# Causal attention in a decoder kernel: a ring of four PSUM banks becomes two tiles of two banks, with one maximum instruction for two heads' pieces

## What is computed

```
q, k, v = layer_norm(x) @ Wqkv + bqkv          # 16 heads of 16 features
s = q @ k.T * 16 ** -0.5                       # per head, 1024 x 1024
s = where(key <= query, s, -inf)
x = x + softmax(s) @ v @ Wout + bout
```

## Time and profile before

| | us |
|---|---|
| median of 3 runs | 1536.88 |
| lowest and highest | 1535.32, 1543.87 |
| the profiled execution | 1545.4 |
| its span | 1543.6 |
| TensorE busy in the span | 1452.9 |
| VectorE busy | 986.8 |
| ScalarE busy | 753.1 |
| GpSimd busy | 494.0 |
| the 304 maxima (L2303), busy | 179.6 |
| the 304 exponentials (L2255), busy | 155.2 |

### The profile page before, as it was taken

The page is one execution under the profiler, slowest core; times in us unless marked ns, Lnnn a source line. Parts: engine busy times, 40 slices in busy tenths (PEclk is TensorE's granted clock), DMA queues, the critical chain, the costliest instruction groups (busy, mean ns, idle before and its releaser), DMA issues. The chain is left out here.

```text
span 1543.6 us, 19029 instructions
## 1 busy us (share of the span) xinstructions
PE 1452.9 (94%) x6910; PEld 848.3 (55%) x6914; DVE 986.8 (64%) x1506; ACT 753.1 (49%) x1237; POOL 494.0 (32%) x410
## 2 busy tenths in 40 slices
PE   6999999989999999888999998898889999999998
PEld 3757764432232265453444443322568888888886
DVE  5774243768877743548888783676677575664853
ACT  5466344443334451543666565434655545445442
POOL 0046420123132410343111112102136655655562
PEclk9999997999999999998999999899999999999999
DMA  7000000000000000083535300000313223223201
GB/s 293 1 0 0 1 1 4 0 1 1 0 1 1 1 0 0 1 164 42 125 51 74 42 3 1 4 1 4 133 42 110 69 83 100 78 74 104 73 10 55
DMA packets 39044, 67.55 MB, mean 44 GB/s; under 512 B 3944, under 2 KB 19368, under 8 KB 38568
## 3 DMA queue, kind: packets, MB, share of 16 engines
q1 hardware_dynamic: 38952, 66.33, 16.1%
HBM read 57.80 MB, written 8.39 MB: 43 GB/s over the span
## 5 line engine op out<-in xcount | busy, mean ns | idle before, releaser
L2255 ACT ACTIVATE arena<-psum 128x512 f32<-128x512 f32 (+1 forms) x304 | 155.2, 583 | 109.9 <-PE psum L2100 109.2
L2303 DVE TENSOR_REDUCE b_mx<-psum 128x1 f32<-128x512 f32 (+3 forms) x304 | 179.6, 650 | 45.0 <-PE psum L2078 36.9
L3047 POOL TENSOR_TENSOR m_w_rest<-m_w,m_w_high 128x512 fp32r<-128x512 f32 (+1 forms) x88 | 111.6, 1270 | 155.6 <-ACT m_w_high L3246 155.6
L3497 DVE TENSOR_TENSOR m_hidden<-m_gelu,psum 128x512 f32<-128x512 f32 (+1 forms) x88 | 60.4, 686 | 148.6 <-ACT m_gelu L3338 124.4
L3140 PE MATMUL psum<-m_x_high,m_w_high 128*128 128x512 f32 (+1 forms) x352 | 138.4, 393 | 3.2 <-issue 3.2
L3053 POOL TENSOR_TENSOR m_h_rest<-m_hidden,m_h_high 128x512 fp32r<-128x512 f32 (+1 forms) x88 | 122.4, 1390 | 58.9 <-ACT m_h_high L3260 58.9
L3140 PE MATMUL psum<-m_x_rest,m_w_high 128*128 128x512 f32 (+1 forms) x352 | 138.0, 392 | 0.0
L3140 PE MATMUL psum<-m_x_high,m_w_rest 128*128 128x512 f32 (+1 forms) x352 | 138.0, 392 | 0.0
L3338 ACT ACTIVATE m_gelu<-psum 128x512 f32<-128x512 f32 (+1 forms) x88 | 52.5, 596 | 120.7 <-PE psum L3140 120.6
L1998 POOL TENSOR_SCALAR_AFFINE_SELECT arena<-arena 128x512 f32<-128x512 f32 x64 | 40.1, 637 | 212.7 <-ACT arena L2255 212.7
L1359 ACT ACTIVATE x_probs<-psum 128x1024 f32<-128x1024 f32 x56 | 57.3, 1024 | 90.9 <-PE psum L1097 90.9
(11 more groups left out here) (591 smaller groups left out, 3238.6 us busy)
## 6 DMA issues: line engine op xcount, KB each, us to landing
m_w<-w SPq DMA_DIRECT2D x32, 512.0 KB, 4.6
m_wo<-wo SPq DMA_DIRECT2D x16, 512.0 KB, 4.0
weights_sb<-weights SPq DMA_DIRECT2D x2, 2820.0 KB, 12.2
m_w<-w SPq DMA_DIRECT2D x16, 344.0 KB, 4.7
b_q_stack<-b_q_dram SPq DMA_DIRECT2D x36, 128.0 KB, 5.9
b_k_stack<-b_k_dram SPq DMA_DIRECT2D x36, 128.0 KB, 6.0
weights_sb<-weights SPq DMA_DIRECT2D x1, 3328.0 KB, 14.0
b_q_dram<-b_q_parts SPq DMA_DIRECT2D x6, 512.0 KB, 3.4
```

The source lines that it names most:

```text
L2255: act.activation(quad_of(g)[:, heads[0]:heads[-1] + 1, 0:n], score(i)[:, 0:len(heads) * n].rearrange("p (h n) -> p h n", n=n), ACT.Exp, sc ...
L2303: dve.tensor_reduce(mx[:, part, qi, heads[0]:heads[0] + nh], tile(("piece", p))[:, 0:nh * keys].rearrange("p (h n) -> p h n", n=keys), AX, ...
L3047: pool.tensor_tensor(w_rest[:, n % W_RING, :, :, 0:H_N(n % HT)], raw_of(n), w_high[:, n % W_RING, :, :, 0:H_N(n % HT)].bitcast(F32), ALU.s ...
L3497: dve.tensor_tensor(hidden[rows, n % 2, :], gelu[rows, n % 2, :], c.bank(2 + n % 2)[rows, :], ALU.mult)\
```

## The change

The ring's four banks become two tiles, each of two neighbouring banks (`c.psum[2]` and `c.psum[3]`); tile n now waits until tile n - 2 is read. A piece may hold twice as many heads, up to four: four at 128 keys (one bank of the tile), four at 256, two at 384 and two at 512. `piece_at` gives the column of a head: as many heads as fit lie side by side in the first bank, the others in the second. One `tensor_reduce` takes the maxima of all heads of a piece. A quad has 20 pieces, 6 of them for its first half, and the layer 160. Shifts, output turns, turns, projections and norm tiles are as before, 512 columns at the start of a tile. The shift follows 3 pieces later in place of 6, and the groups ahead of the first slot are pieces 0 to 1, 2 to 3 and the rest. `count_pieces` is unchanged and adds up the new sizes.

```diff
-    SCORES, TILES = 3, 4
+    SCORES, TILES = 3, 2
...
-    LATER = 6
+    LATER = 3
...
-        ring_bank = lambda what: c.bank(SCORES + 1 + nth[what] % TILES)
+        ring_pair = lambda what: c.psum[(SCORES + 1) // 2 + nth[what] % TILES]
+        ring_bank = lambda what: ring_pair(what)[:, 0:CH]
...
-                    bank = tile(("piece", p))
+                    tile(("piece", p))
+                    to = ring_pair(("piece", p))
                     diagonal = first + keys == (qi + 1) * P
                     for x, h in enumerate(heads):
-                        mm = pe.matmul(bank[:, x * keys:(x + 1) * keys], qs[n % 3][0:ROWS, h, qi * P:(qi + 1) * P],
+                        at = piece_at(x, keys)
+                        mm = pe.matmul(to[:, at:at + keys], qs[n % 3][0:ROWS, h, qi * P:(qi + 1) * P],
                                        ks[n % 3][0:ROWS, h, first:first + keys], start=True, stop=not diagonal)
                         if diagonal:
-                            mm = pe.matmul(bank[:, (x + 1) * keys - P:(x + 1) * keys], ident16, future[:], start=False, stop=True)
+                            mm = pe.matmul(to[:, at + keys - P:at + keys], ident16, future[:], start=False, stop=True)
...
-                more_pieces(0, 4)
+                more_pieces(0, 2)
                 later_value(2)
-                more_pieces(4, 8)
+                more_pieces(2, 4)
                 later_value(3)
-                more_pieces(8, upto[0])
+                more_pieces(4, upto[0])
...
-                    dve.tensor_reduce(mx[:, part, qi, heads[0]:heads[0] + nh],
-                                      tile(("piece", p))[:, 0:nh * keys].rearrange("p (h n) -> p h n", n=keys), AX, ALU.max)\
-                       .then_inc(s["read"].sem)
+                    tile(("piece", p))
+                    each = piece_at(1, keys)
+                    scores_of = ring_pair(("piece", p))[:, 0:nh * each].rearrange("p (h n) -> p h n", n=each)[:, :, 0:keys]
+                    dve.tensor_reduce(mx[:, part, qi, heads[0]:heads[0] + nh], scores_of, AX, ALU.max).then_inc(s["read"].sem)
...
+def piece_at(x, keys):
+    a_bank = CH // keys
+    return x // a_bank * CH + x % a_bank * keys
...
-            per = min(QUAD, CH // n)
+            per = min(QUAD, 2 * (CH // n))
```

## The result

| | before | after |
|---|---|---|
| median of 4 runs, us | 1540.38 | 1558.16 |
| lowest and highest | 1535.32, 1546.26 | 1554.33, 1560.3 |
| profiled execution, us (span) | 1545.4 (1543.6) | 1554.33 (1552.6) |

What follows compares the result with a forecast made beforehand. The prediction took TensorE to bound the long middle and VectorE the short start. Start -0.5, middle +17 and end +0.7 summed to about +17 us on 1536.88, forecasting 1554 us, with a range of 1536 to 1566.

Steps and rivals of the forecast that it cites:

- The bound: Short start bound by VectorE, long middle by TensorE; VectorE has 4.4 us of slack per quad there.
- The merger's saving: Each of 144 merged maxima saves VectorE 0.07 us, 10 us in all; only more slack in the middle.
- The waits of the middle: TensorE waits for tiles in the two-tile ring: net +2.5 us per quad, +17 us over the middle.
- Slots 4 and 5: In a half's slots 4 and 5, a pair waits 0.1 us and scores catching up with ScalarE's exponentials cost 0.2.
- The quad with turns and projections: Middle quad with the first batch's turns and projections: +2 us, as projections are long and VectorE has time.
- The start: Up to the second quad's first pieces: -0.5 us as a whole, with -2 and +3 as ends.
- The end: After the last maxima: a last pair ends 0.7 us later, +0.7 us; later turns and projections add 0.
- the waits are absorbed: Rival: small holes in TensorE's queue and earlier maxima absorb the middle's waits; about +2 us, 1539; chance 0.17.
- VectorE's pace holds TensorE: Rival: from 700 us to the second quad's first pieces, VectorE holds TensorE; -12 us, 1525; chance 0.07.
- The clock rival: Rival: idle clumps in middle quads drop TensorE's granted clock to 0.67; +12 us on top, 1566; chance 0.04.

Runs made afterwards that it cites:

- added maxima: Kernel before, with four more 512-column maxima per quad into a tile nobody reads; 1543.35 us, ratio 1.0044.
- run with the GpSimd wait: Changed kernel, with GpSimd's subtraction for the second batch entry's keys waiting until VectorE has made the first shift; 1557.24 us, ratio 1.0135.
- half-read maxima: Changed kernel, with maxima over two-bank pieces reading only half of each head's keys, omitting the others; 1533.55 us, ratio 0.9988.
- order-alone run: Changed kernel's order on every queue, with the four one-bank tiles and one-bank maxima of the kernel before; 1536.14 us, ratio 1.0005.
- run with small tiles of two banks: Changed kernel's order with one-bank pieces and maxima in the four-bank ring, but each small tile taking two banks; 1552.51 us, ratio 1.0119.

## Why the prediction was right, point by point

**The bound** was read rightly: taking VectorE work away gained nothing in the middle, and adding 2.4 us per quad cost 0.53. VectorE's slack is not as free as I put it, since the ring couples the two.

**The merger's saving** of 0.07 us per pair is there. Three items queued behind each other, and then three pairs:
```profile
779.19 2.95 DVE L2309 TENSOR_REDUCE b_mx<-psum 128x2 f32<-128x1024 f32 x3 [0.97 <-PE psum L2078]
...
784.75 3.49 DVE L2309 TENSOR_REDUCE b_mx<-psum 128x2 f32<-128x1024 f32 x3 [0.54 <-PE psum L2078]
```
(3.49 - 1.22) / 2 is a pitch of 1.13 us, as taken. The changed kernel and its run with two instructions per pair show it directly: VectorE is busy for 24.28 and 25.46 us of a period, 1.18 us for 18 mergers. Between the kernel before and the changed one the busy time for maxima fell by 7.2 us only, for the 10 of the sum and the 18 by what I quoted of the Trainium skill's VectorE page; what took the other 3, no run shows.

**The waits of the middle** came out one by one:

| place | forecast, us | measured, us |
|---|---|---|
| 4 x 128 piece behind two pairs | 0.35 | 0.39 |
| shift behind it | 0.65 | 0.65 |
| output turn | 0.3 | 0.34 |
| pair behind it | 0.45 | 0.42 |
| shift of the first half | 0.65 | 0.65 |
| pair behind that | 0.2 | 0.20 |

The last two are from this stretch of TensorE in the changed kernel:
```profile
770.47 0.22 PE L2081 MATMUL psum<-b_future,ident 128*128 128x128 bf16 x1
771.18 0.39 PE L2088 MATMUL psum<-ident,b_shift 128*8 128x128 bf16 x4 [0.49 <-DVE b_mx L2309]
771.50 0.50 PE L2103 MATMUL psum<-weights_sb 98*128 98x384 bf16 x2
772.04 0.34 PE L2078 MATMUL psum<-b_k_stack,b_q_stack 96*128 96x384 bf16 x1
```
The last mask is 0.06 us long in a row, so the shift could start at 770.53; the two scores of 0.17 us end at 771.84 and the pair starts at 772.04. They add to 2.65 us for the 2.6 forecast, and the period grew by 2.85 for a forecast of 2.5. The rest is in small terms that all fell the same way. Slots 4 and 5, put at 0.3 us, measure 0.35, and one wait was on no list of mine, a pair behind the output turn of the first half:
```profile
775.21 0.63 PE L2127 MATMUL psum<-ident,ln 128*128 128x128 f32 x4 [0.27 <-ACT ln L2266]
775.81 0.39 PE L2078 MATMUL psum<-b_k_stack,b_q_stack 96*128 96x512 bf16 x1
...
792.25 0.60 PE L2103 MATMUL psum<-weights_sb 98*128 98x512 bf16 x2
792.80 0.60 PE L2078 MATMUL psum<-b_k_stack,b_q_stack 96*128 96x512 bf16 x2
793.24 0.90 PE L2103 MATMUL psum<-weights_sb 98*128 98x384 bf16 x3
793.98 0.60 PE L2078 MATMUL psum<-b_k_stack,b_q_stack 96*128 96x512 bf16 x2
```
The four transposes take 0.44 us in a row, so the pair at 775.81 is 0.16 us late, where the piece in its place was 0.02 late before. At 792.80 it is 0.11, and at 793.98, behind three scores that take 0.50 us in a row, 0.24. From all this go about 0.35 us of waits that TensorE had before and has no more; I had taken 0.4 off.

**The quad with turns and projections** was put at +2 and is +2.96: the reason given for its being lighter, the long projections, didn't hold, and no run took that quad apart. The second quad, which I counted among the six, grew 2.96 as well. The middle is +20.2 us for +17.

**The start** was put at -0.5 and is +0.6. The part up to the first scores was put at +0.5 and measures +0.1: 699.90 - 683.64 = 16.26 us before and 689.58 - 673.19 = 16.39 after, as the copy had waited 0.17 us for the transposes before and the GpSimd operation happened to end 0.14 us sooner after the first piece. What failed is the gain behind it: from the first scores to the first marker 16.5 us became 17.0, where 1.1 of gain less 0.4 was expected. The mean granted clock in that stretch is 0.60 for 0.75, and at the low level a pair takes longer to fill, which I had only as an end of the range; that the clock is the whole cause was not tried.

**The end** was put at +0.7 and is +1.6, for another reason than the one given. The wait for the last shift did grow, by 0.43 us (2.17 for 1.74, where I gave 2.4), but what it grew by lies ahead of the last marker: from there to the shift's transposes it is 0.74 us for 0.78. The growth is behind the shift, and it is the clock, which neither this term nor its bounds had. Before:
```profile
928.58 1.67 PE L2115 MATMUL psum<-arena,weights_sb 128*32 128x512 f32 x13
```
and after, with the windows of that stretch:
```profile
938.65 0.33 PE L2088 MATMUL psum<-ident,b_shift 128*8 128x128 bf16 x3 [2.17 <-DVE b_shift L2323]
...
938.87 3.18 PE L2118 MATMUL psum<-arena,weights_sb 128*32 128x512 f32 x13
```
```profile
936.50:938.60 2.10, 0.00 (x0) 0.00 (x0) 1.90 (x5) 0.33 (x1) 1.13 (x2) 1.00 0.00 0
938.60:942.00 3.40, 3.35 (x21) 1.03 (x21) 1.61 (x3) 0.00 (x0) 0.00 (x0) 0.54 0.01 2
```
These 13 matmuls span 3.18 us in place of 1.67, at a granted clock of 0.54; before it was 1.00 there. That is 1.5 of the 1.6 us.

**The rivals.** That the waits are absorbed fell with the period; that VectorE's pace holds TensorE fell with the added maxima. The clock rival didn't happen in the middle, where the changed kernel's granted clock is 1.00 from 712 to 938 us, but it did at both ends: behind the changed kernel's last shift, and in the second quad of the run with the GpSimd wait and of the run with two instructions per pair.

**The number.** The sum was 17 us, and the layer grew by 22.4: the middle is 3 us over, the start and the end 1 us each, all to the same side. The 17.8 us between the two medians of the result lie closer to the sum than it deserves, since the median of before stood high in these four executions; against the later sessions the difference is 22 us as well. The time, 1554 us for 1558.16, is 4 us low because the sum was. The mechanism and the places of the waits were right, the two ends of the layer were not.

## What to carry to other kernels

A ring's depth is counted in tiles, and every small item counts as one: before making tiles larger, write down for each item what stands the ring's depth ahead of it, and when that is given back. Fewer and larger instructions on an engine with slack buy nothing, and a longer hold on a shared tile is paid by the engine that has none. Such a count by hand, from the distances of the trace and the order in the code, gave each of six waits within 0.05 us here, and missed one of 0.14 that was not on the list.

## What the runs showed of the hardware that I had not expected

- One idle stretch of TensorE of about 2 us can cost its clock, and need not. The 13 matmuls behind the last shift take 1.67 us at full speed. After 1.74 us of idle time they did so in three kernels, the kernel before among them, and took 3.12 in a fourth (the half-read maxima). After 2.02 us they took 2.95 in the order-alone run and 1.67 in the run with small tiles of two banks; after 2.17 to 2.30 us they took 2.92 to 3.18 in all five kernels. The order-alone run adds 0.28 us of waiting there, and from the last marker to the next layer it takes 49.95 us where the kernel before takes 48.48: a small wait came with 1.5 us more, and in the run with small tiles of two banks, with the same wait, with nothing (48.44 us).
- A VectorE operation of 0.17 us from SBUF to SBUF stood for 3.90 us beside a GpSimd tensor_tensor that had started 0.19 us ahead of it, while maxima that read PSUM ran beside the same operations at their usual 0.6 us; a wait on GpSimd that moves its operation out of the way made the whole kernel 0.3% faster.
